# First mixture of an audio tower: where the silus of a tile go and who sums them, and which operand of the second product stands still

## The reference, cut to what matters

```python
h = silu(einsum('td,efd->tef', x, w1))            # 16 experts, F = 512
h_sum = einsum('tef,te->ef', h, mask)             # sum over the tokens of an expert
h_mean = h_sum / maximum(counts, 1)[:, None]
y_mean = einsum('ef,edf->ed', h_mean, w2)         # 16 x 128
out = einsum('tk,tkd->td', routing_w, y_mean[top_idx])
```

## Time and profile before

| | |
|---|---|
| time, median of 3 runs | 2127.57 us (2126.83 to 2128.0) |
| the profiled execution | 2145.36 us, span 2143.6 us |
| PE busy | 1903.3 us (89%) |
| DVE busy | 1673.4 us (78%) |
| ACT busy | 1385.0 us (65%) |
| POOL busy | 1349.7 us (63%) |

### The profile page before, as it was taken

The page is one execution under the profiler, slowest core; times in us unless marked ns, Lnnn a source line. Parts: engine busy times, 40 slices in busy tenths (PEclk is TensorE's granted clock), DMA queues, the critical chain, the costliest instruction groups (busy, mean ns, idle before and its releaser), DMA issues.

```text
span 2143.6 us, 50732 instructions
## 1 busy us (share of the span) xinstructions
PE 1903.3 (89%) x17146; PEld 1367.5 (64%) x17146; DVE 1673.4 (78%) x4764; ACT 1385.0 (65%) x2070; POOL 1349.7 (63%) x1026
## 2 busy tenths in 40 slices
PE   7999510588998997799999999999999999999998
PEld 5565400246566985567777777777777777777776
DVE  4586741583566866879999999999999999999998
ACT  3112442561443554578888888888888888888886
POOL 2110067103890002278898989898988889888887
PEclk8799755797998996599999999999999999999999
DMA  3512073530330002000000100000200000000000
GB/s 90 167 41 108 30 244 128 102 71 30 94 118 1 1 0 82 1 2 2 0 0 0 54 28 1 0 0 1 80 2 0 0 0 1 2 10 10 10 10 18
DMA packets 73497, 82.63 MB, mean 39 GB/s; under 512 B 38564, under 2 KB 56516, under 8 KB 71684
## 3 DMA queue, kind: packets, MB, share of 16 engines
q1 hardware_dynamic: 70660, 75.19, 11.6%
q0 software_dynamic: 2688, 5.44, 0.7%
HBM read 42.97 MB, written 29.20 MB: 34 GB/s over the span
## 4 chain that ended last, share of the span: by engine, by line
PE 56%; DVE 3%; issue 1%; POOL 0%; ACT 0%; ACTq 0%; DVEq 0%; POOLq 0%
PE bank L2339 29%; PE bank L2322 27%; DVE m_work L2212 1%; DVE m_best L2209 0%; DVE m_work L2203 0%; DVE m_ut L792 0%; PE bank L2291 0%; DVE m_best L2202 0%; DVE m_ex L2214 0%; ACT m_h L2153 0%; DVE h L2250 0%; POOL m_h L2098 0%; DVE m_red L2215 0%; PE bank L784 0%; DVE m_row L2195 0%
## 5 line engine op out<-in xcount | busy, mean ns | idle before, releaser
L2339 PEld LDWEIGHTS bank<-weights,m_h 128*128 128x128 f16 x10752 | 639.3, 98 | 189.8 <-DVE hc L2241 77.7
L2098 POOL TENSOR_TENSOR m_h<-m_hidden,m_h 128x896 f16<-128x896 f32 x384 | 725.0, 1888 | 31.9
L2241 DVE SCALAR_TENSOR_TENSOR hc<-bank,m_shares,hc 128x128 f32<-128x128 f32 x2688 | 727.0, 341 | 4.3 <-PE bank L2339 4.3
L2339 PE MATMUL bank<-weights,m_h 128*128 128x128 f16 x10752 | 724.3, 219 | 2.4 <-POOL m_h L2098 2.4
L2150 ACT ACTIVATE m_hidden<-bank,m_b 128x896 f32<-128x896 f32 x384 | 386.7, 1007 | 184.3 <-PE bank L2322 184.3
L2228 DVE TENSOR_TENSOR m_h<-bank,m_h 128x896 f16<-128x896 f32 x384 | 419.2, 1092 | 108.8 <-ACT m_h L2153 108.8
L2096 POOL TENSOR_SCALAR m_h<-m_hidden 128x896 f16<-128x896 f32 x384 | 359.8, 937 | 111.7 <-ACT m_hidden L2150 79.0
L2322 PE MATMUL bank<-m_u_first,weights 128*128 128x448 f16 (+1 forms) x1536 | 417.4, 354 | 7.2 <-DVE h L2250 5.5
L2322 PE MATMUL bank<-m_u_second,weights 128*128 128x448 f16 (+1 forms) x1536 | 417.2, 353 | 0.0
L2147 ACT ACTIVATE bank<-bank,m_b 128x896 f32<-128x896 f32 x384 | 377.3, 982 | 0.4 <-PE bank L2322 0.4
L2153 ACT ACTIVATE m_h<-bank 128x896 f16<-128x896 f32 x384 | 348.8, 908 | 0.0
(11 more groups left out here) (328 smaller groups left out, 2177.2 us busy)
## 6 DMA issues: line engine op xcount, KB each, us to landing
weights<-expert_factors SPq DMA_DIRECT2D x12, 1024.0 KB, 8.1
expert_slots<-lru_zeros SPq DMA_DIRECT2D x1, 8256.0 KB, 31.9
lw_raw<-e_w_dram SPq DMA_DIRECT2D x16, 512.0 KB, 4.9
expert_factors<-lw_made SPq DMA_DIRECT2D x16, 512.0 KB, 4.9
ew_raw<-e_w_dram SPq DMA_DIRECT2D x16, 512.0 KB, 4.4
lru_wst<-w_dram SPq DMA_DIRECT2D x16, 256.0 KB, 2.8
weights<-w_dram SPq DMA_DIRECT2D x1, 4096.0 KB, 12.7
expert_factors<-ew_made SPq DMA_DIRECT2D x8, 512.0 KB, 3.1
```

What stands on the lines that cost most here:

```text
L2098: g.tensor_tensor(h1[:, x, 1], hidden[:, x], h1[:, x, 0], ALU.subtract).then_inc(second_of[1], 1)
L2241: last = v.scalar_tensor_tensor(acc[:, m * TW:(m + 1) * TW], y[q][:, (n - start) * TW:(n - start + 1) * TW], shares[:, m, e:e + 1], acc[:, ...
L2339: last = t.matmul(y[q][:, (n - start) * TW:(n - start + 1) * TW], factors[:, m, n * TW:(n + 1) * TW], k.weights[:, grp % 2, 2 + m, at], st ...
```

## The change

In the tile loop, the first set of a tile (quarters 0 and 1) goes as before. The silu of the second set goes from PSUM to SBUF, into one of two buffers `later_half`, which are views of the tiles `rows` and `left` that the routing no longer needs. DVE sums quarter 2 from there. Of quarter 3 POOL first adds the upper 192 columns onto the lower 192, and DVE sums those 192, one place later in its order. PE may write the second set again when its silu is done, and ACT waits for the sums of the tile before last before it writes a buffer. DVE has three reductions in a tile, of 768, 384 and 192 columns, in place of two of 768.

In the second product the block of weights (128 x 128) is stationary and a single column of `hsum` moves; each expert's four matmuls accumulate in one column of a 128 x 16 result. `hsum` shrinks to 128 x 4 x 16 and POOL's memset goes. The result is copied to SBUF, transposed by PE, and copied to `ym`.

```diff
+        later_half = [t[:].rearrange("p n e -> p (n e)")[:, 0:FP * ST].rearrange("p (f n) -> p f n", f=FP) for t in (rows, left)]
 (POOL)
-            g.memset(hsum[:], 0.0).then_inc(made, 1)
+            for j in range(NST):
+                pool.wait_ge(later_silu, j + 1)
+                fold = later_half[j % 2][:, 1]
+                g.tensor_tensor(fold[:, 0:ST // 2], fold[:, 0:ST // 2], fold[:, ST // 2:], ALU.add).then_inc(folded, 1)
 (ACT)
-            for j in range(PARTS * NST):
-                act.wait_ge(up, j + 1)
-                sc.activation(set_banks(j), set_banks(j), ACT.Silu).then_inc(silu, 1)
+            for j in range(NST):
+                act.wait_ge(up, PARTS * j + 1)
+                sc.activation(set_banks(2 * j), set_banks(2 * j), ACT.Silu).then_inc(silu, 1)
+                act.wait_ge(up, PARTS * j + 2)
+                if j >= 2:
+                    act.wait_ge(later_summed, j - 1)
+                    act.wait_ge(fold_summed, j - 1)
+                sc.activation(later_half[j % 2], set_banks(2 * j + 1), ACT.Silu).then_inc(later_silu, 1)
 (DVE)
-            for j in range(PARTS * NST):
+            def fold_sum(j):
+                dve.wait_ge(folded, j + 1)
+                v.tensor_reduce(part[:, j, FC - 1:FC], later_half[j % 2][:, 1:2, 0:ST // 2], X, ALU.add).then_inc(fold_summed, 1)
+
+            for j in range(NST):
                 dve.wait_ge(silu, j + 1)
-                v.tensor_reduce(part[:, j // PARTS, j % PARTS * FP:(j % PARTS + 1) * FP], set_banks(j), X, ALU.add).then_inc(summed, 1)
+                v.tensor_reduce(part[:, j, 0:FP], set_banks(2 * j), X, ALU.add).then_inc(summed, 1)
+                if j:
+                    fold_sum(j - 1)
+                dve.wait_ge(later_silu, j + 1)
+                v.tensor_reduce(part[:, j, FP:FC - 1], later_half[j % 2][:, 0:1], X, ALU.add).then_inc(later_summed, 1)
+            fold_sum(NST - 1)
...
-            v.tensor_copy(ym[:], k.bank[0:E0, 7, 0:128]).then_inc(y_kept, 1)
+            v.tensor_copy(y_cols[:], k.bank[:, 7, 0:E0]).then_inc(y_copied, 1)
+            dve.wait_ge(y_turned, 1)
+            v.tensor_copy(ym[:], k.bank[0:E0, 6, 0:128]).then_inc(y_kept, 1)
 (PE)
-                        pe.wait_ge(summed, n - SETS + 1)
+                        pe.wait_ge(later_silu if n % PARTS else summed, (n - SETS) // PARTS + 1)
...
-            for f in range(FC):
-                for x in range(E0):
-                    last = t.matmul(k.bank[0:E0, 7, 0:128], hsum[:, f, x * E0:(x + 1) * E0], w2[:, x, f, :],
-                                    start=(x == 0 and f == 0), stop=(x == E0 - 1 and f == FC - 1))
+            for x in range(E0):
+                for f in range(FC):
+                    last = t.matmul(k.bank[:, 7, x:x + 1], w2[:, x, f, :], hsum[:, f, x:x + 1], start=(f == 0), stop=(f == FC - 1))
             last.then_inc(y_ready, 1)
+            pe.wait_ge(y_copied, 1)
+            t.transpose(k.bank[0:E0, 6, 0:128], y_cols[:], k.ident[:]).then_inc(y_turned, 1)
```

More of the change, by code:

```diff
@@ L842, in first_mixture @@
         part_t = sb("part_t", [NST, FC * 128])
-        hsum = sb("hsum", [128, FC, E0 * E0])
+        hsum = sb("hsum", [128, FC, E0])
+        y_cols = sb("y_cols", [128, E0])
         ym = sb("ym", [E0, 128])
         xt = sb("xt", [128, RING, 2, ST], F16)
+        later_half = [t[:].rearrange("p n e -> p (n e)")[:, 0:FP * ST].rearrange("p (f n) -> p f n", f=FP) for t in (rows, left)]
         rt = k.hc[0:E0, :]
@@ L867, in first_mixture @@
         summed = sem("silu_summed")
+        later_silu = sem("later_silu_ready")
+        later_summed = sem("later_summed")
+        folded = sem("quarter_folded")
+        fold_summed = sem("fold_summed")
         parts_turned = sem("tile_sums_turned")
@@ L872, in first_mixture @@
         y_ready = sem("y_ready")
+        y_copied = sem("y_columns_copied")
+        y_turned = sem("y_turned")
         y_kept = sem("y_kept")
@@ L912, in _ @@
             g.memset(going[:], 1.0).then_inc(made, 1)
-            g.memset(hsum[:], 0.0).then_inc(made, 1)
             g.iota(line[:], [[1, NST]], base=0, channel_multiplier=0, allow_small_or_imprecise_dtypes=True).then_inc(made, 1)
             g.iota(tile_no[:], [[0, 1]], base=0, channel_multiplier=1, allow_small_or_imprecise_dtypes=True).then_inc(made, 1)
-            pool.wait_ge(made, 6)
+            pool.wait_ge(made, 5)
             g.memset(going[:, :, 0:1], 0.0).then_inc(made, 1)
@@ L993, in _ @@
             link(v.tensor_scalar(absent[:], mask[:], -BIG, BIG, ALU.mult, ALU.add))
-            dve.wait_ge(made, 8)
+            dve.wait_ge(made, 7)
             dve.wait_ge(ranked, 1)
@@ L1045, in _ @@
             dve.wait_ge(by_expert, 1)
-            v.tensor_copy(hsum[:, :, 0:E0 * E0:E0 + 1], k.bank[:, 1, 0:FC * E0].rearrange("p (f e) -> p f e", f=FC)).then_inc(gathered, 1)
+            v.tensor_copy(hsum[:], k.bank[:, 1, 0:FC * E0].rearrange("p (f e) -> p f e", f=FC)).then_inc(gathered, 1)
             dve.wait_ge(y_ready, 1)
-            v.tensor_copy(ym[:], k.bank[0:E0, 7, 0:128]).then_inc(y_kept, 1)
+            v.tensor_copy(y_cols[:], k.bank[:, 7, 0:E0]).then_inc(y_copied, 1)
+            dve.wait_ge(y_turned, 1)
+            v.tensor_copy(ym[:], k.bank[0:E0, 6, 0:128]).then_inc(y_kept, 1)
             for c in range(NCW):
@@ L1065, in _ @@
             pe.wait_ge(counted, 1)
-            pe.wait_ge(made, 8)
+            pe.wait_ge(made, 7)
             for q in range(2):
@@ L1093, in _ @@
             pe.wait_ge(k.w2_in, 16)
-            pe.wait_ge(summed, PARTS * NST)
+            pe.wait_ge(later_summed, NST)
+            pe.wait_ge(fold_summed, NST)
             for f in range(FC):
```

## The result

The changed kernel takes 2139.04 us (median of 4 runs, 2138.48 to 2142.01) against 2127.2 us before (2123.84 to 2128.0): a ratio of 1.0054, 95% interval 1.0028 to 1.0081, or 11.8 us slower. The forecast was 2135.9 us, 8.3 us slower.

What follows compares the result with a forecast made beforehand. DVE was taken to bound the tile loop, with everything after it on the path; loop -5.4, transposes to product +0.3, second product +10.9, turn +0.9, output product +1.6 sum to +8.3 us: 2135.9 us, range 2123 to 2147.

Runs made afterwards that it cites:

- e6: Changed kernel plus 16 unread 512-column float16 matmuls in PE's idle times between loop and second product; 2136.61 us against 2127.66 before, ratio 1.0041.

## What to carry to other kernels

Before letting the operand with few columns move, look for what the clock does: a float32 stream of 128-column loads with one moving column lasted as long as one with 128 at the same clock (0.11 us a record at 1.00, 0.21 at 0.50), and it lost the full clock here. When an engine is relieved, ask of the next one not only how long its instructions are but what its sequencer does between them; an idle time marked "issue" that comes once in every turn of a loop can be such work, and it became the bound here without any engine looking busy. A total that scatters by 15 us can't tell 3 us; the stage in the trace can.

## What was not expected of the hardware

- Adding 127 useless moving columns to each of 64 matmuls made them 11.6 us faster (27.46 to 15.89 us), through the clock alone.
- 512-column matmuls in idle time brought the product's start to 1.00, but in the stream of one-column matmuls it fell to 0.50 after 1.6 us (e6).
- The same n1, n3 and output product run at different clocks from one execution to the next: n1 at 0.50 in one profile and 1.00 in 13, n3 at 0.50 in three, the output product in 13.6 or 16.5 us behind the same second product.
- From a tile's last weight load to the next tile's first, the register load costs the sequencer 0.7 us in all, of which the load itself is 0.30. Without bounds at the load, the loop went from 73 to 126 us.
